# Halves of Wq at the head of both DMA queues, and a new order of the first loads, in a gated attention and FFN block

## What is computed

```python
def _L0_xattn_ref(q, k, v, Wq, Wk, Wv):
    qh = jnp.einsum('bse,he->bsh', q, Wq)
    kh = jnp.einsum('bse,he->bsh', k, Wk)
    vh = jnp.einsum('bse,he->bsh', v, Wv)
    scores = jnp.einsum('bqh,bkh->bqk', qh, kh) / jnp.sqrt(jnp.float32(HEAD))
    causal = jnp.tril(jnp.ones((seqd, seqd), dtype=bool))
    scores = jnp.where(causal, scores, -jnp.inf)
    probs = jax.nn.softmax(scores, axis=1)
    return jnp.einsum('bqk,bkh->bqh', probs, vh)

def _L0_ffn_ref(x, clip_x, clip_down, w_gate, w_up, w_down):
    xq = _act_fake_quant(x, clip_x[0])
    gate = jnp.einsum('bsh,ih->bsi', xq, _weight_fake_quant(w_gate))
    up = jnp.einsum('bsh,ih->bsi', xq, _weight_fake_quant(w_up))
    h = _act_fake_quant(jax.nn.silu(gate) * up, clip_down[0])
    return jnp.einsum('bsi,hi->bsh', h, _weight_fake_quant(w_down))

x = x + jnp.tanh(g_xattn[0]) * _L0_xattn_ref(_layernorm(x, axis=-1), ctx_1024, ctx_1024, Wq, Wk, Wv)
x = x + jnp.tanh(g_ffn[0]) * _L0_ffn_ref(_layernorm(x, axis=-1), clip_x, clip_down, w_gate, w_up, w_down)
```

## Time and profile before

| | us |
|---|---|
| median of three runs | 113.39 |
| the profiled execution, its own time | 113.61 |
| its span, first to last instruction | 111.8 |
| TensorE busy with matmuls | 103.4 (93%) |
| VectorE busy | 84.5 (76%) |
| ScalarE busy | 70.0 (63%) |
| GpSimd busy | 50.9 (46%) |
| inputs moved by DMA | 9.44 MB read |

### The profile page before, as it was taken

One profiled execution on the slowest core, in us unless ns is written; L12 is line 12 of the kernel. 1 busy time (PEld: TensorE's weight loads), 2 busy tenths in 40 slices (PEclk: granted clock), 3 DMA queues, 4 the chain that ended last, 5 costly groups with the idle time before them and its releaser, 6 DMA issues.

```text
span 111.8 us, 1835 instructions
## 1 busy us (share of the span) xinstructions
PE 103.4 (93%) x614; PEld 79.7 (71%) x616; DVE 84.5 (76%) x209; ACT 70.0 (63%) x132; POOL 50.9 (46%) x85
## 2 busy tenths in 40 slices
PE   5979999999999999999999989999999799799960
PEld 2258888988889898898998977444444498677740
DVE  0274295697889959759559979659999997989992
ACT  0321252469864576645887978689888870999400
POOL 7214035073460815525066283046687631599910
PEclk9999999999999999999999999999999999999997
DMA  3998999998000000000000000000000000005555
GB/s 45 361 380 215 375 416 427 410 407 333 16 0 0 3 0 0 6 0 3 0 0 0 0 0 6 0 0 3 0 0 0 6 0 0 0 12 196 181 181 186
DMA packets 5513, 11.65 MB, mean 104 GB/s; under 512 B 640, under 2 KB 2688, under 8 KB 5504
## 3 DMA queue, kind: packets, MB, share of 16 engines
q1 hardware_dynamic: 4928, 10.75, 26.4%
q10 hardware_dynamic: 576, 0.79, 2.2%
HBM read 9.44 MB, written 2.10 MB: 103 GB/s over the span
## 4 chain that ended last, share of the span: by engine, by line
PE 51%; DVE 25%; DMA 6%; ACT 6%; POOL 4%; issue 4%; ACTq 1%; DVEq 0%; POOLq 0%
PE ps L450 13%; PE ps L472 11%; PE ps L498 9%; DVE hmax L1116 8%; DMA wvT<-in_wvT 6%; DVE ps L1148 4%; DVE xs L1152 4%; DVE shared L1111 3%; PE ps L508 2%; PE ps L510 2%; PE ps L509 2%; PE ps L658 2%; POOL shared L412 2%; PE ps L519 2%; POOL xn L401 2%
## 5 line engine op out<-in xcount | busy, mean ns | idle before, releaser
L658 PE MATMUL ps<-xq,wguT 128*128 128x512 bf16 x78 | 17.2, 379 | 0.1
L412 POOL TENSOR_TENSOR shared<-up_sb,silu 128x1024 f32<-128x1024 f32 x5 | 11.8, 2364 | 10.6 <-ACT up_sb L857 10.6
L658 PEld LDWEIGHTS ps<-xq,wguT 128*128 128x128 bf16 x80 | 7.8, 98 | 9.2 <-DVE shared L1111 0.2
L450 PE MATMUL ps<-wvT,shared 128*128 128x256 f32 x56 | 13.3, 380 | 0.2 <-DMA wvT<-in_wvT 0.2
L472 PE MATMUL ps<-shared,a_sb 128*128 128x256 f32 x56 | 13.2, 379 | 0.0
L1116 DVE TENSOR_REDUCE hmax<-shared 128x1 f32<-128x2048 f32 (+1 forms) x6 | 12.7, 2108 | 0.6 <-POOL shared L412 0.2
L362 POOL TENSOR_SCALAR var<-mv 128x2 f32<-128x2 f32 x8 | 1.5, 193 | 24.8 <-DVE mv L948 24.6
L852 ACT ACTIVATE silu<-ps,gu_scale 128x1024 f32<-128x1024 f32 x10 | 11.1, 1114 | 2.4 <-PE ps L658 2.4
L450 PEld LDWEIGHTS ps<-wvT,shared 128*128 128x128 f32 x56 | 10.6, 190 | 2.0 <-issue 0.6
L498 PE MATMUL ps<-uT,shared 128*128 128x256 f32 (+1 forms) x64 | 11.9, 329 | 0.0
L705 PE MATMUL ps<-wdT,hq 128*128 128x256 bf16 x80 | 11.0, 273 | 0.6 <-DVE hq L1163 0.5
(11 more groups left out here) (141 smaller groups left out, 217.4 us busy)
## 6 DMA issues: line engine op xcount, KB each, us to landing
shared<-in_xc SPq DMA_DIRECT2D x6, 512.0 KB, 10.8
out<-xs SPq DMA_DIRECT2D x7, 256.0 KB, 2.2
xs<-in_x SPq DMA_DIRECT2D x3, 512.0 KB, 8.4
shared<-in_wgu SPq DMA_DIRECT2D x3, 512.0 KB, 7.9
shared<-in_xc SPq DMA_DIRECT2D x4, 256.0 KB, 6.2
wd<-in_wd SPq DMA_DIRECT2D x1, 768.0 KB, 12.1
wq_sb<-in_wq ACTq DMA_DIRECT2D x1, 256.0 KB, 4.1
wk_sb<-in_wk SPq DMA_DIRECT2D x1, 256.0 KB, 3.9
```

Of the source, the lines that this page charges most:

```text
L412: nc.gpsimd.tensor_tensor(hid[:, 2 * i + 1, :], up_sb[i % 2][:], silu1[i % 2][:], ALU.mult).then_inc(hid_done[1], 1)
L450: last = nc.tensor.matmul(bank2(VB[b])[:, k, :], ctxT(b)[:, e, k * P:(k + 1) * P], weights[:, e, :], start=(e == 0), stop=(e == KT - 1))
L658: last = nc.tensor.matmul(bank(4 * half + 2 * g + c), wguT[:, i, g, k, :], xq[:, k, col:col + CH], start=(k == 0), stop=(k == KT - 1))
```

## The change

Each DMA queue now begins with one half of Wq (128 KB): half 0 on SyncE's queue, half 1 on ScalarE's. On SyncE's queue follow Wk, `ctxT(0)`, `xT(0)` (these two in exchanged order), the rows of batch 1, `xT(1)` and `ctxT(1)`. On ScalarE's queue follow Wv, the rows of batch 0 (these two in exchanged order) and the scalars. VectorE waits for each half by a semaphore of its own. One of the ten products of ones at the start is left out.

```diff
-WARM_AT_START = 10
+WARM_AT_START = 9
...
-        wq_here = sem("wq_here")
+        wq_here = [sem(f"wq_here{h}") for h in range(KT)]
...
+            sp.dma_start(wq_sb[:, 0], wq_in[:, 0]).then_inc(wq_here[0], 16)
             sp.dma_start(wk_sb[:], wk_in).then_inc(wk_here, 16)
+            sp.dma_start(ctxT(0), xc_in[0, :, 0]).then_inc(c_here[0], 16)
             sp.dma_start(xT(0), xc_in[0, :, 1]).then_inc(xT_here[0], 16)
-            sp.dma_start(ctxT(0), xc_in[0, :, 0]).then_inc(c_here[0], 16)
             load_x(1)
...
-            act.dma_start(wq_sb[:], wq_in).then_inc(wq_here, 16)
+            act.dma_start(wq_sb[:, 1], wq_in[:, 1]).then_inc(wq_here[1], 16)
+            act.dma_start(wvT[:], wvT_in).then_inc(wv_here, 16)
             act.dma_start(xs[:, 0:QT, :], x[:, 0:QT, :]).then_inc(x_here[0], 16)
-            act.dma_start(wvT[:], wvT_in).then_inc(wv_here, 16)
...
-            dve.wait_ge(wq_here, 16)
             for h in range(KT):
+                dve.wait_ge(wq_here[h], 16)
                 nc.vector.bn_stats(bnq[:, h, :], wq_sb[:, h, :]).then_inc(bnq_done, 1)
```

## The result

| | before | changed |
|---|---|---|
| median, us | 113.29 | 114.19 |
| lowest and highest of 6 runs each | 113.25, 113.50 | 113.79, 114.42 |
| span of the profiled execution | 111.8 | 112.3 |

The ratio is 1.0073, with a 95% interval of 1.0053 to 1.0092: the changed kernel is **slower by 0.7%**, 0.9 us. 112.7 was predicted, with 113.5 as the upper end. The profiled execution of the changed kernel took 114.13 us against 113.61 before, so the two traces show 0.5 us of the 0.9.

The account below looks back on a forecast made before the run. Bound by TensorE's stream, whose start waits on early DMA landings. L482 at 9.36 instead of 10.04 gains 0.68 us: 113.39 - 0.68 = 112.7 us, range 112.1 to 113.5.

Parts of the forecast that it names:

- Step 4: Spreading of deviations (L482, changed L483): rows land 7.1, deviations ready 9.21, TensorE stalls 0.4 us, start 9.36 instead of 10.04.
- both bounds: Each landing by KB on its own queue and by KB of both queues at equal shares; rows 7.3 and 6.9.
- step 6: SyncE's queue: one more issue, 0.45 us nobody waits for; later loads issued 2.5 us earlier, only filling the lull.
- Step 1: VectorE starts on half 0 of Wq at 4.0 instead of 4.86; TensorE waits for Wk (5.3), starts at 5.43.
- Step 2: TensorE's values could start at 7.25; the wait for Wv at 8.24, about 0.4 us long, is gone.
- Step 3: Values and queries f = 0 take 0.86 us each, L482 could start at 8.97; `xT(0)`, needed at 8.11, there by 7.95.
- Step 5: From L482 on nothing is closer than before; scores come 2.17 us later, at 11.53, so `scores(0)` starts 0.68 us earlier.
- Step 7: Start of TensorE: one warming product less, 0.43 us while it waits, hidden at both lengths.
- the rows land where Wv did: Rows of batch 0, third on ScalarE's queue, land at 8.1; L482 at 10.38, 0.34 us slower, 113.7; chance 0.04.
- The clock rival: TensorE's clock rises later, so real work starts at half rate: 0.6 to 1.4 us slower, about 114.3; chance 0.08.

Follow-up runs that it names:

- late release: Changed kernel with SyncE's wait ahead of its later loads for the rows of batch 0 instead of Wv: 113.38 us; with ten warming products too, 113.21 us.
- early release: SyncE's wait ahead of its later loads for Wk instead of Wv: 113.18 us on the kernel before, 113.07 us on the changed kernel with rows ahead of Wv.
- second profile: The changed kernel itself, run and profiled once more with no edit: 113.98 us, ratio to before 1.0026 to 1.0108.
- Wq whole: Changed kernel with Wq in one piece at the head of ScalarE's queue, both new orders and nine warming products kept: 113.94 us.
- before, nine products: Kernel before with nine warming products instead of ten, nothing else: 113.36 us.

## Why the prediction was wrong

**Step 4 failed, by the size of one term.** The mechanism was foreseen: "With the rows landed at 7.1 they are ready at 9.21 ... This is what is late next." TensorE did stall there, and for that reason. But the rows landed at 8.3, in both profiles, and the way from there to L483 was 2.3 us (2.26 predicted). All of the difference between 9.36 and 10.58 is in the landing. It was bounded to 6.9 to 7.3, and both bounds shared an assumption: that the queues go on as they had in the kernel before, with 367 GB/s over this stretch. They moved 250. The rate alone does not make the error, since Wq, Wk and Wv came sooner than forecast: with the late release the two profiles have 307 and 305 GB/s, and rows at 7.2 and 7.1, where they were forecast. What was missing from the 7.1 is the term of step 6.

**Step 6 failed, and it is the root of the other.** It costed the 2.5 us earlier issue of the later loads at nothing: "behind the early ones on the same queue, and only fill the lull". The release at 5.04 instead of 8.12 is what the late-release runs take back, at the rows 1.1 us with nine products (8.3 twice, against 7.2) and 0.8 with ten (7.9 against 7.1). That price holds with Wv ahead of the rows; with the rows ahead an early release cost nothing (113.07, and 113.18 in the kernel before). So the term is one of the order and the release together. It was looked at as a cost to SyncE and to the order of one queue, not as a load on the DMA engines while ScalarE's third transfer was under way. The Trainium skill (DMA: Bandwidth & Descriptors, Issuing engines are not separate DMA queues) says that the transfers of all issuing engines run on the same DMA engines and interleave; that bears on this step and was not drawn on for it. The trace agrees in that the packets of both queues took time of the 16 engines over 4.5 to 8 us: SyncE's queue 58.6%, ScalarE's 32.6%. The page does not explain why the sum of the rates falls, which the runs show.

**The rest, point by point.** Step 1: VectorE started at 3.56 (4.0 predicted) and Wk landed at 4.7 (5.3); L558 at 5.11 was bound by the ninth product, not by Wk. Step 2: right; L451 started at 7.07 (7.25) and no longer waited for a DMA. Step 3: `xT(0)` at 8.5 instead of 7.95 at most made a wait of 0.42, hidden behind the larger one here; in the second profile it landed at 9.4, with a wait of 1.21, hidden too, but by no more than 0.2 us. Step 5: right; from L483 to the scores it was 2.18 (2.17 predicted), and nothing was lost or gained up to the end. Step 7: its cover was thin. The product was called hidden at both lengths, and in the ten runs of the changed kernel, none above 114.42, nothing speaks against it. In two kernels near it, with nine products, one run of six and four of ten took longer by 1.4 to 2 us.

**The rivals.** That the rows land where Wv did was given 0.04, at 113.7. The landing came out so, with 8.3 for 8.1 and L483 at 10.58 for 10.38, but not for the reason given: the rows stand third with the late release too, and land at 7.2. "Against: 128 KB less stands ahead" counted KB, where the rate was what changed. The clock rival was given 0.08, at 0.6 to 1.4 us. Where runs of a kernel fell apart, the upper group lay 1.4 us above the rest on the mean (Wq whole), and the one at 115.40 2 us above (before, nine products), but the real work of those kernels begins at 6.0 and not at 5.1, so this does not test the price here. The clock did not make the loss of the changed kernel's profiled executions, where L558 took 2.12 and 2.21 instead of 1.98, and that was hidden behind the wait for the rows.

**The reference of the sum.** In the profiled execution of before Wv landed at 8.1. In the two other profiles with its orders and whole Wq (early release, and nine products) it was 7.9 and 7.8, and L482 started at 9.89 and 9.76. So the profiled execution was a late one by 0.15 to 0.3 us, as its 113.61 beside the median of 113.29 says too; that, with the 0.54 of the traces, makes most of the 0.9 measured. The prediction allowed for it, by taking its 0.68 off the median instead of 113.61; but the gain, too, is reckoned from that late start, 10.04. A start at 9.36 gives 112.9 (an estimate: 9.36 and 103.55), so the 112.7 was too low by 0.2 by its own steps.

**What stays open.** What holds the DMA rate down. Over 4.5 to 8 us it was low in each of the seven profiles with Wq in halves and Wv second on its queue (250 to 307 GB/s), and in none of the other profiles (336 to 380). But the stretch begins with a dip that all twelve profiles with halves have, nine of them before any later load was issued; the early release of the kernel before had one too, without halves and before its release at 4.50 (242 and 152 GB/s over 3 to 4 us). What is peculiar to the seven is that the rate does not recover, and an early release makes that worse: over 5.5 to 8 us 242 to 306 GB/s, 325 and 326 with the late one, 360 to 388 in halves with the rows ahead of Wv. Over 4.5 to 8 us ScalarE's queue moved 0.26 MB in 32.6% of the engines' time, before 0.48 MB in 42.2%; SyncE's 0.61 MB in 58.6%, before 0.80 MB in 61.1%. So the packets of both queues took longer, ScalarE's most. The views used here have the rate per queue and not per DMA engine, so whether some engines run ahead into the later loads while others keep the landing waiting could not be seen, and no run here tests it.

## What to carry to other kernels

A transfer that is moved down a queue can be late by more than the KB put ahead of it, when the move also pulls forward a wait that holds back other loads: look at what each landing releases, and keep such a throttle tied to the last operand that is needed, not to one that the change makes early. Here this was worth 1.1 us at the landing in one order of the loads and nothing in another, so it wants a run of its own. When a chain of DMAs feeds two engines, the operand with the longest way behind it (here the rows, 2.3 us through VectorE and GpSimd) wants the place ahead of the one that is used at once. And a piece of filler on TensorE that looks hidden in one profile should be tried over many executions, since the clock's rise does not come at the same moment in each.

## What was not expected of the hardware

**The rise of TensorE's clock wanders.** The warming products begin at 1.30 in every profile. Of the 18 profiles, the last ones ran at 2.4 GHz in seven, from about 4 to 4.9 us on. In the other eleven all of them ran at 1.2 GHz, and the rise fell within or behind the real work: L558 took from 2.08 to 2.72 us where 1.98 is full rate, and 3.75 with Wq whole and nine products, where 0.7 us of idle time stood between. The Trainium skill (TensorE: Matmul & The Clock Gate, Part 1) gives half a microsecond to either side for this from run to run. Here it was from about 4 us to some 7 us, and some 10 us in the run with the idle time, so the measurement decides. Starting the real work sooner therefore gains less than it seems: in the thirteen profiles with its start at 5.1 to 5.6 instead of 6.04, part of it ran at half rate in ten.

**The first transfers land sooner when they are smaller, by more than their share.** 128 KB on each queue landed at 3.2 to 3.9 in all profiles with halves, 256 KB at 4.2 to 5.0: about 1.1 us sooner. The interpolation had 0.8. What is won there is in part lost again in the dip that follows over 4 to 5 us.
